# Decoder of two layers on one core: a third stage buffer for the expert weights, six weight slices held back on GpSimd, the first ternary matrix moved to an earlier place

## What is computed

```python
x = x + _L0_attn_ref(_layernorm(x), Wqkv, Wo)            # 16 heads of 16, rotary, causal
x = x + _L0_xattn_ref(_layernorm(x), ctx_2048)           # product with a context, fp8-rounded operands
x = x + _L0_ffn_ref(_layernorm(x), Wg, W1, W3, W2, Ws1, Ws3, Ws2)   # 16 experts + shared, 4 chosen
x = x + _L1_attn_ref(_layernorm(x), w_qkv, w_proj)       # ternary weights, 8-bit activations
x = x + _L1_xattn_ref(_layernorm(x), tokens, ctx, ctx, ctx)  # 4 experts chosen by a hash of the token
x = x + _L1_ffn_ref(_layernorm(x), w_gate, w_up, w_down, ln_weight) # ternary gated layer, width 1024
...
def _weight_quant(w):                                    # the ternary form
    s = 1.0 / jnp.clip(jnp.mean(jnp.abs(w)), 1e-05)
    return jnp.clip(jnp.round(w * s), -1.0, 1.0) / s
```

## Time and profile before

| what | value |
|---|---|
| median of three executions | 683.1 us |
| the profiled execution | 683.42 us |
| its span | 681.6 us |
| mean granted TensorE clock | 0.975 |
| TensorE matmul busy | 586.2 us (86%) |
| VectorE busy | 416.4 us (61%) |
| ScalarE busy | 298.4 us (44%) |
| GpSimd busy | 124.7 us (18%) |
| transfers | 8.5% of 16 engines' span in the main queue |

### The profile page before, as it was taken

One profiled execution on the slowest core, in us unless ns is written; L12 is line 12 of the kernel. 1 busy time (PEld: TensorE's weight loads), 2 busy tenths in 40 slices (PEclk: granted clock), 3 DMA queues, 4 the chain that ended last, 5 costly groups with the idle time before them and its releaser, 6 DMA issues.

```text
span 681.6 us, 11559 instructions
## 1 busy us (share of the span) xinstructions
PE 586.2 (86%) x4703; PEld 399.8 (59%) x4746; DVE 416.4 (61%) x993; ACT 298.4 (44%) x470; POOL 124.7 (18%) x162
## 2 busy tenths in 40 slices
PE   2588768889999889998899999999999987888776
PEld 1334434446776567776667777677767645546444
DVE  3568896883557655368525664337545673566585
ACT  2325236337541167512566225771349537532443
POOL 2246054230000410000140000400004010120442
PEclk9799999999999899999979999999999999998969
DMA  6036022110000100000001000010020000000000
GB/s 214 0 123 264 1 98 58 41 62 1 1 2 1 62 1 1 2 1 1 0 15 50 1 2 1 1 62 1 1 93 2 1 1 0 1 1 16 0 16 31
DMA packets 5408, 21.03 MB, mean 31 GB/s; under 512 B 843, under 2 KB 3019, under 8 KB 4460
## 3 DMA queue, kind: packets, MB, share of 16 engines
q1 hardware_dynamic: 5356, 20.30, 8.5%
HBM read 19.25 MB, written 1.05 MB: 30 GB/s over the span
## 4 chain that ended last, share of the span: by engine, by line
PE 58%; DVE 27%; ACT 8%; issue 5%; DMA 1%; POOL 0%; SPq 0%; ACTq 0%; DVEq 0%
PE ps L883 18%; PE ps L914 16%; DVE nmx L1657 4%; PE ps L657 4%; ACT L1354 2%; PE ps L771 2%; PE ps L893 2%; PE ps L679 1%; DVE y L1554 1%; PE ps L712 1%; PE ps L752 1%; PE ps L744 1%; PE ps L707 1%; PE ps L641 1%; ACT hs L1354 1%
## 5 line engine op out<-in xcount | busy, mean ns | idle before, releaser
L1766 DVE TENSOR_TENSOR hs<-hs,ps 128x512 f32<-128x512 f32 (+1 forms) x68 | 45.5, 669 | 103.7 <-PE ps L883 57.9
L914 PE MATMUL ps<-w2f,hs 128*128 128x256 f32 x400 | 101.0, 397 | 0.0
L1354 ACT ACTIVATE hs<-ps 128x512 f32<-128x512 f32 (+1 forms) x68 | 39.7, 584 | 119.9 <-PE ps L883 119.6
L914 PEld LDWEIGHTS ps<-w2f,hs 128*128 128x128 f32 x400 | 73.1, 192 | 18.4 <-issue 9.6
L641 PE MATMUL ps<-selh,idb 128*128 128x512 bf16 x314 | 74.4, 379 | 2.5 <-issue 1.1
L504 POOL TENSOR_TENSOR ve<-mv,half 128x2 f32<-128x2 f32 x24 | 4.7, 196 | 381.9 <-DVE mv L1547 381.9
L1657 DVE TENSOR_REDUCE nmx<-ps 128x2 f32<-128x512 f32 (+1 forms) x96 | 61.0, 680 | 6.1 <-PE ps L712 5.7
L641 PEld LDWEIGHTS ps<-selh,idb 128*128 128x128 bf16 x334 | 31.2, 98 | 35.8 <-issue 2.1
L1313 ACT ACTIVATE pk<-ps 128x512 f32<-128x512 f32 x64 | 34.7, 595 | 18.3 <-PE ps L755 18.1
L1354 ACT ACT_TABLE_LOAD x33 | 42.3, 1283 | 0.6
L883 PE MATMUL ps<-yah,w3h 128*128 128x256 f16 x200 | 39.1, 278 | 3.7 <-DVE hs L1772 3.7
(11 more groups left out here) (234 smaller groups left out, 1184.2 us busy)
## 6 DMA issues: line engine op xcount, KB each, us to landing
stage<-in_w SPq DMA_DIRECT2D x8, 800.0 KB, 4.2
tstage<-in_tern SPq DMA_DIRECT2D x4, 1024.0 KB, 4.8
w2f<-in_w SPq DMA_DIRECT2D x1, 3200.0 KB, 14.2
cs<-in_ctxT SPq DMA_DIRECT2D x1, 1024.0 KB, 10.2
cd<-in_ctxT SPq DMA_DIRECT2D x1, 1024.0 KB, 4.6
out_x<-xs SPq DMA_DIRECT2D x4, 256.0 KB, 2.2
w0s<-in_w SPq DMA_DIRECT2D x1, 768.0 KB, 6.8
xs<-in_x SPq DMA_DIRECT2D x1, 768.0 KB, 8.1
```

The source lines that it names most:

```text
L914: mm = pe.matmul(ps[:, bank, j * D:(j + 1) * D], hs[:, n % 4, par * S + j * P:par * S + (j + 1) * P], w, start=(first and par == 0 and j = ...
L1354: act.activation(hs[:, n % 4, 0:w], ps[:, gate_bank(n), 0:w], ACT.Silu).then_inc(e_sil.sem, 1)
L1766: TT(hs[:, n % 4, 0:w], hs[:, n % 4, 0:w], ps[:, up_bank(n), 0:w], ALU.mult).then_inc(e_hb.sem, 1)
```

## The change

The stage has three buffers in use and the transfers go round them in turn (slice q into buffer q mod 3, for q = 2b + n), so the first three slices wait for nothing and each later one for the slice three before; the transfer of w2 now stands before the fourth slice. On GpSimd a wait for `m_ok` = 2, which ScalarE signals when the maxima of iteration 1 have been read back, stands before slice (1, 0); the router's scaling for batch 0 comes between (1, 0) and (1, 1), and the rest of the slices follow without other work between them. `ternary(0)` moves in front of the scaling for the context of iteration 2. On ScalarE the copies (1, 0), (1, 1) and (2, 0) stand in the second part of iteration 0, (2, 1), (3, 0) and (3, 1) in the first part of iteration 1, the last of them before the turned queries; the magnitudes of the first ternary matrix follow the third exponentials of iteration 2.

```diff
--- before.py
+++ after.py
@@ -341,7 +341,7 @@
         d_w0 = sig("d_w0")
         d_ctx = sig("d_ctx")
         d_sel = sig("d_sel")
-        d_wst = [sig(f"d_w{n}", 16) for n in (1, 3)]
+        d_wst = [sig(f"d_wst{n}", 16) for n in range(3)]
         d_ts = sig("d_ts", 16)
         d_lnw = sig("d_lnw")
         d_cd = sig("d_cd")
@@ -473,13 +473,13 @@
             sp.dma_start(tki[:, :], tok).then_inc(d_sel.sem, 16)
             sp.dma_start(sels[0:33, :], sel0).then_inc(d_sel.sem, 16)
             sp.wait_ge(w0_lo.sem, 2)
-            for b in range(B):
-                if b == 1:
+            for q in range(2 * B):
+                b, n = divmod(q, 2)
+                if q == 3:
                     sp.dma_start(w2f[:, :], w2).then_inc(d_w2.sem, 16)
-                for n, w in enumerate((w1, w3)):
-                    if b:
-                        sp.wait_ge(wst_lo.sem, wst_lo.at(b - 1, n + 1))
-                    sp.dma_start(stage[:, n, :], w[:, b * W_SLICE:(b + 1) * W_SLICE]).then_inc(d_wst[n].sem, 16)
+                if q >= 3:
+                    sp.wait_ge(wst_lo.sem, q - 2)
+                sp.dma_start(stage[:, q % 3, :], (w1, w3)[n][:, b * W_SLICE:(b + 1) * W_SLICE]).then_inc(d_wst[q % 3].sem, 16)
             sp.wait_ge(wst_lo.sem, 2 * B)
             for n in range(4):
                 if n:
@@ -509,7 +509,8 @@
                 g.wait_ge(wst_hi.sem, wst_hi.at(b, n + 1))
                 for a in range(0, W_SLICE, LOW_PIECE):
                     cols = slice(b * W_SLICE + a, b * W_SLICE + a + LOW_PIECE)
-                    last = g.tensor_tensor(wl[n][:, cols], stage[:, n, a:a + LOW_PIECE], wh[n][:, cols], ALU.subtract)
+                    last = g.tensor_tensor(wl[n][:, cols], stage[:, (2 * b + n) % 3, a:a + LOW_PIECE], wh[n][:, cols],
+                                           ALU.subtract)
                 last.then_inc(wst_lo.sem, 1)
 
             step = [0]
@@ -585,18 +586,19 @@
                 split_lo(0, n)
             rsqrt_ln("context", 0)
             rsqrt_ln("head", 2)
+
+            g.wait_ge(m_ok.sem, 2)
             split_lo(1, 0)
+            rsqrt_ln("router", 0)
             split_lo(1, 1)
-            rsqrt_ln("router", 0)
-            for n in range(2):
-                split_lo(2, n)
-            split_lo(3, 0)
+            for b in range(2, B):
+                for n in range(2):
+                    split_lo(b, n)
             rsqrt_ln("context", 1)
             rsqrt_ln("head", 3)
-            split_lo(3, 1)
             rsqrt_ln("router", 1)
+            ternary(0)
             rsqrt_ln("context", 2)
-            ternary(0)
             rsqrt_ln("head", 4)
             rsqrt_ln("router", 2)
             rsqrt_ln("context", 3)
@@ -1329,11 +1331,12 @@
 
             def slices(b, n):
 
-                act.wait_ge(d_wst[n].sem, 16 * b + 16)
+                act.wait_ge(d_wst[(2 * b + n) % 3].sem, 16 * ((2 * b + n) // 3) + 16)
                 if b == 1 and n == 0:
                     act.wait_ge(c_done.sem, 1)
                     act.wait_ge(c_lo.sem, 1)
-                act.activation(wh[n][:, b * W_SLICE:(b + 1) * W_SLICE], stage[:, n, :], ACT.Copy).then_inc(wst_hi.sem, 1)
+                act.activation(wh[n][:, b * W_SLICE:(b + 1) * W_SLICE], stage[:, (2 * b + n) % 3, :],
+                               ACT.Copy).then_inc(wst_hi.sem, 1)
 
             def magnitudes(n):
 
@@ -1400,15 +1403,21 @@
                 exponentials(it, 2)
                 if it == ITS - 1:
                     silu(0, 0)
-                if it < 2:
-                    slices(2 * it, 0)
+                if it == 0:
+                    slices(0, 0)
+                if it == 1:
+                    slices(2, 1)
+                if it == 2:
+                    magnitudes(0)
                 sil(it, 2)
                 if routes:
                     router_exp(it - 1)
                 exponentials(it, 3)
                 stacks(it + 1, 0)
-                if it < 2:
-                    slices(2 * it, 1)
+                if it == 0:
+                    slices(0, 1)
+                if it == 1:
+                    slices(3, 0)
                 sil(it, 3)
                 if it == ITS - 1:
                     silu(0, 1)
@@ -1416,27 +1425,26 @@
                 sil(it, 4)
                 stacks(it + 1, 1)
                 exponentials(it, 5)
+                if it == 1:
+                    slices(3, 1)
                 if it == ITS - 1:
                     squares(0)
                     down(0)
                 turned_queries(it + 1, 0)
                 sil(it, 5)
                 turned_queries(it + 1, 1)
-                if it == 1:
-                    slices(3, 0)
-                if it == 2:
-                    magnitudes(0)
                 sil(it, 6)
 
             def phase_b0(it):
                 sil(it, 7)
                 split_hi("output", it, yTh[:, :, :])
-                if it < 2:
-                    slices(2 * it + 1, 0 if it == 0 else 1)
+                if it == 0:
+                    slices(1, 0)
+                    slices(1, 1)
                 sil(it, 8)
                 quantised("context", it)
                 if it == 0:
-                    slices(1, 1)
+                    slices(2, 0)
                 sil(it, 9)
                 if it:
                     router_turned(it - 1)
```

## The result

| | before | changed |
|---|---|---|
| median (executions) | 683.38 us (6) | 674.58 us (6) |
| lowest to highest | 682.59 to 686.07 | 673.43 to 679.84 |
| profiled execution, its span | 683.42, 681.6 us | 679.84, 678.0 us |
| mean granted clock in it | 0.975 | 0.970 |

The ratio is 0.9894, 95% interval 0.9858 to 0.9930: 1.1% faster. The profiled execution is of the upper group. The profile under *e3* is the same kernel from the lower one (span 672.7 us, clock 0.990), and the two together show the change better than either.

A forecast was written before the change was run, and what follows sets the result against it. TensorE (58% of the chain) was taken as the bound, VectorE (27%), stretched beside GpSimd, as the second. +0.75 - 4.20 + 0.35 = -3.1 us gave 680.3, or 680.0 us on the median; range 676.5 to 684.0.

The forecast's parts named there:

- part 3: Iteration 1 beside a GpSimd cutting without pause: VectorE loses net 1.7 us, ScalarE's copy adds 0.9; +1.7 at the stacks.
- the last step, from the sum to the median: Profiled 683.4 us less the sum gives 680.3; it lay 0.3 above the median, so the forecast is 680.0 us.
- iteration 2's first scores: Start of iteration 2: expected at +0.75 us; as a sign, within 1 us of their time before.
- the collision's end: End of iteration 2: without GpSimd's `ternary(0)` beside VectorE's xs addition, the window shortens by 4.20 us.
- new place of `ternary(0)`: Iteration 2: `ternary(0)` and its magnitudes cost 0.35 us there, bounds 0 and 2.5.
- Part 1: End of iteration 0: six slices leave, VectorE gains 3.3 us; the turn waiting for xs comes about 2.3 us earlier.
- Part 2: Behind the new wait: router scaling and normalisations end later, 0.9 of 2.3 us left; slice transfers, with three buffers, cost nothing.
- Part 4: End of iteration 1: VectorE gains about 2.1 us, dummies cap TensorE's gain at 0.96; iteration 2 starts at +0.75 us.
- Part 5: `ternary(0)` and its magnitudes moved in iteration 2: 4.20 us gained at the old place, 0.35 us paid at the new.
- iteration 1 is cheaper than priced: Rival: tiny router instructions slip through and TensorE does not wait for the router's scaling; -5.7, 677.4 us; chance 0.24.
- slower: Rival: every exposed VectorE instruction in iteration 1 waits a whole GpSimd instruction, 9.4 us instead of 2.9; 687.4 us; chance 0.08.
- Everything is given back: Rival: iteration 1 pays 3 us more than priced, or `ternary(0)`'s new place costs 2.5 us; 683 us; chance 0.22.

The follow-up runs named there:

- e3: The changed kernel run again unchanged, to see how far its executions differ; 675.94 us, ratio 0.9924.
- e4: The changed kernel with GpSimd's new wait on `m_ok` left out; 678.18 us, ratio 0.9927.
- e10: The changed kernel with the router's scaling ahead of slice (1, 0), still behind the wait; 679.76 us, ratio 0.9942.
- e9: The changed kernel with eight clock-keeping matmuls ahead of the turned first norm of layer 1 in iterations 3 and 4; 676.36 us, ratio 0.9892.
- e7: The kernel before, unchanged, one execution more with its profile; 682.12 us.
- e8: The changed kernel with each weight slice cut in eight instructions of 200 columns instead of four of 400; 680.70 us, ratio 0.9973.

## Why the prediction was wrong

In short: part 3 charged iteration 1 with 1.7 us that were not lost, so that the sum is -4.85 and not -3.1 us; and the last step, from the sum to the median, put the clock's changes between executions at nothing, where 2.5 us more lie. The second is what carries the time out of the range.

By its own steps, each read in e3 beside the profile of before, less the 0.95 us by which e3 already leads at the first reading (43.82 - 42.87):

| point | predicted | measured |
|---|---|---|
| router's turn in iteration 1 (L636) | -0.9 | 101.68 - 103.86 + 0.95 = -1.2 |
| first stacks there, without the copy | +0.8 | 116.91 - 119.17 + 0.95 = -1.3 |
| the copy of slice (3, 1) | +0.9 | 119.43 - 120.91 + 0.95 + 1.3 = +0.8 |
| iteration 2's first scores | +0.75 | 145.14 - 147.74 + 0.95 = -1.65 |
| the collision's end | -4.20 | 9.95 - 14.33 = -4.4 |
| new place of `ternary(0)` | +0.35 | 0 (interval 2: 81.06 for 81.05) |
| low clock behind 243.65 | none | about +1.2 |
| sum | -3.1 | -4.85 |

**Part 1** stood: the turn that waits for xs was to come 2.3 us earlier and came 2.4 (96.44 - 99.83 + 0.95). What the wait on `m_ok` adds to the new order is not shown (e4).

**Part 2** stood in the pair for the router (1.96 for 2.03 us) and its sum was 0.3 us too dark. Its line "with three buffers there are 5 us or more" held: 5.4 us from the release (98.7) to ScalarE's read (104.11) in e3. With a transfer of 4.2 us in between, only 1.2 us are in hand. To cost that at nothing was right for the kernel as it is; with the slice cut later, in e10, ScalarE waits.

**Part 3 is the step that failed.** It charged 1.7 us for iteration 1's VectorE beside a GpSimd that cuts without pause, at half an instruction for each meeting. From the router's turn to the first stacks it measured about 0 (-1.2 to -1.3). VectorE's rows of e3:

```profile
102.91 0.96 DVE L1720 TENSOR_TENSOR rr<-rA,rB 128x512 f32<-128x512 f32 x1
...
108.87 0.39 DVE L1735 TENSOR_TENSOR prob<-lex,lrc 128x32 f32<-128x32 f32 x1
...
109.78 0.36 DVE L1741 COPY gt<-gm 128x12 f32<-128x12 f32 x1
...
110.58 0.45 DVE L1745 TENSOR_TENSOR gs<-gm,gr 128x8 f32<-128x8 f32 x1
111.06 0.17 DVE L1746 TENSOR_SCALAR gs<-gs 128x8 f32<-128x8 f32 x1
...
113.36 1.06 DVE L1720 TENSOR_TENSOR rr<-rA,rB 128x512 f32<-128x512 f32 x1
```

The first rotation lost 0.27 us (0.69 free). Of the four tiny instructions the product lost 0.20, the copy 0.19, the comparison 0.28 (0.19, 0.17 and 0.17 free, in iteration 2) and the minus one nothing: 0.67 us where I had charged four times 0.45. Part of this was there before: the product took 0.42 us in the kernel before too, which the prediction did not count, so 0.71 us of these 0.94 are new. The second rotation starts at 113.36 for 115.20, which is -0.9 us by the table's count, so only 0.3 us reached it; and it gained 0.43 on the 1.49 of the earlier trace rows. The price read from the earlier trace rows, 0.6 to 0.8 us for an instruction, comes from instructions that meet a slice singly. In the chain of short ones each lost less than half of that, and more than half of the new loss did not reach the rotation. The rule of the Trainium skill, "SBUF — State Buffer", section "Who interferes with whom", that a copy or scalar form in a two-port mode waits for the whole GpSimd instruction, agrees in kind with the trace for the copy (0.36 for 0.17 us). My price, half a GpSimd instruction for each of the four, was 2.7 times what they lost.

**Part 4** was right about the limit: the router's weights are turned 1.1 us earlier relative to the second pair of stacks (142.97 against 145.58 before), close to the 0.96 us at which the dummies were said to cap it. Its end was wrong only by what part 3 handed on.

**Part 5** gained its 4.2 us (4.4), and the new place costs nothing at TensorE, although VectorE does pay there: the rotation at 174.81 takes 1.68 us and the stack part at 177.13 1.39 us. The step lacked the question that the first part of the prediction asked of the old place: what does TensorE's clock do after a wait? Ten microseconds later, at 243.65, stands a wait of 1.89 us. It was there before, with the clock full behind it; now the clock falls there. From iteration 3's first scores to its end it is 316.03 - 235.31 = 80.7 us in e3 and was 321.83 - 242.28 = 79.55 us: 1.2 us given back, about 1 of them to that clock (e9).

**The rest is the clock, as far as the profiles go.** Taken off the profile's own 683.4 us, 4.85 us give 678.6, inside the range. The medians are 7.3 us apart (65 executions of the kernel before in all the runs, 683.3 us, beside 675.9). What is left is about 2.5 us. In the profiles, what differs beyond the steps above is low-clock stretches that come and go between executions of one kernel: the earlier trace rows's kernel had 2.6 us of them in iteration 4 alone, which e7 does not have. Which executions take which stretch I can't say, nor why the kernel before takes more; a line fitted through time and clock puts the two kernels 5.5 us apart at equal clock, 0.98. This stays open. I had read the profile's sum against its own time and then treated the median as if it stood 0.3 us below for every kernel. That the median fell near a rival's figure is luck of the same kind: the steps alone do not give it.

The rival "iteration 1 is cheaper than priced" (677.4 us, down to 675.7 with all of it) came half true. Its first condition held: the tiny instructions cost the path almost nothing, and its argument, that a pair of router instructions lost 0.63 us together and not each, was a measurement. Its second did not: the router's scaling is what TensorE waits for (1.10 us at 101.68, behind VectorE's 1.26 us for `rstd`), so 1.2 of the 2.3 us stayed, as part 2 had said. Half-way from -3.1 to -7.4 is moreover -5.25 and not -5.7 us, and the 2.9 us in "slower" is worked out nowhere. "Everything is given back" and "slower" did not occur.

One of the signs failed, and it depends on the execution: iteration 2's first scores were to stay within 1 us. In e3 they come 1.65 us earlier, in the changed kernel's own profile, with the low clock in iteration 1, 2.0 us later (149.66 - 147.74, and 0.11 for the first reading), by which alone a reader would have picked the wrong rival. The others stood, but for the last of the four tiny instructions (0.17 us).

## What to carry to other kernels

Price a meeting of a VectorE and a GpSimd instruction by the kind of chain it stands in: here long instructions that met a piece of 400 columns singly lost 0.3 to 1.3 us each, and four short ones in a chain 0.67 us together. When a wait is taken off TensorE, look at the next long wait behind it, even one that was harmless before (1.89 us here), since the clock can fall there instead. And before a difference of 1% between two profiles is explained, take the lengths of the untouched stages in at least two profiles of the same kernel: here 3.5 of the 8.9 us between the spans of before and e3 were no part of it, 2.6 in interval 4 and 0.95 ahead of the first reading.

## What the runs showed of the chip

- Equal waits of TensorE (1.29 and 1.45 us, at 117.77 and 116.91 us) left the granted clock at 1.00 in one execution and at 0.72 over the next 12 us in another, 3.7 us of difference for the same kernel. The Trainium skill, "TensorE: Matmul & The Clock Gate", section "What's actually happening", says that the number of slow matmuls at a kernel's start varies from run to run; these two profiles show the like in the middle of one.
- A GpSimd subtraction in pieces of 200 columns made the held slices of 1600 columns 4.2 to 5.4 us long (e8), in pieces of 400 3.7 to 4.4 us (changed and e3). Slice (0, 1), cut earlier, took 7.1 us for 3.7.
- The reduction over the partitions of `ternary(0)` is followed by 7.58 us in which GpSimd waits for nothing that the profile shows, and by 6.89 us at the old place, where 5.80 us of the same kind stand ahead of it too. Whether the reduction itself runs on in that time the rows do not tell. Here nothing waited for it; where the result is urgent, it is a term of its own. First the changed kernel, then before:

```profile
166.95 0.45 POOL L527 PARTITION_ALL_REDUCE aall<-asum  x1 [12.85 <-ACT absj L1348]
174.97 0.18 POOL L528 TENSOR_TENSOR wsc<-aall 128x1 f32<-128x1 f32 x1 [7.58 <-issue]
```

```profile
223.12 0.18 POOL L527 TENSOR_TENSOR wsc<-aall 128x1 f32<-128x1 f32 x1 [6.89 <-issue]
```
